# Rotary position step of a gated Mamba and MoE block: the halves of queries and keys change places by SBUF transfers instead of a TensorE product

## The chip, the cores and the metric

The kernel runs on one core of one Trainium2 chip. The metric is the time of one execution in microseconds (us), as the device measures it; the median of several runs is given. The engines of the core are TensorE (PE in the profile; PEld is its weight load), VectorE (DVE), ScalarE (ACT), GpSimd (POOL) and SyncE (SP), which here only issues DMA transfers (SPq). Each engine works through its own list of instructions in order, and waits on semaphores.

## The reference

Four sequences of 512 tokens with 512 channels go through two stages, each behind a tanh gate:

```
x = x + tanh(g_xattn) * mamba(ctx, z=layernorm(x))     # 16 states, 512 channels
x = x + tanh(g_ffn)   * block(layernorm(x))
block(x):
    h = rms(x) ;  q = h@wq + bq ;  k = h@wk + bk ;  v = h@wv + bv     # 16 heads of 32
    q, k = q*cos + rot(q)*sin, k*cos + rot(k)*sin     # rot(t) = concat(-t2, t1), halves of 16
    x = x + causal_attention(q, k, v) @ wo
    x = x + MoE(rms(x))        # 8 experts, top 2, and a shared expert
```

`rot` is the step that changes: within each head of 32 channels the first 16 and the last 16 change places, one of them with its sign turned.

## The kernel before

The program is written engine by engine: five functions, one for each engine, list its instructions, and counting semaphores join them. There is no scheduler; the order in the text is the order on each engine.

After `first_scan` (the Mamba scan of sequence 0) there are four rounds, `round_(b, s)` with b = 0 to 3 and s = b + 1. Round b does the attention of sequence b and, in rounds 0 to 2, the scan of sequence s beside it. Round 3 has no scan; it does the first pieces of the shared expert instead (`last_units`). Then the MoE stage follows.

Within a round there are three stretches: norms and transposes; then the **rotary stretch**, a loop over eight tiles m = 0 to 7 (four of queries, four of keys, each 128 channels by 512 tokens, so four heads in the partitions); then the 16 `units` of attention with the 64 scan blocks spread between them. The rotary stretch is where the change lies. For each tile m, in the kernel before:

- PE `product(b, m)`: 12 matmuls of line 631 into one of two PSUM banks;
- ACT `bias(b, m)`, line 1296: adds the bias and writes the tile into `QB[:, m % 2]`, one of two buffers (in `EX`), once tile m - 2 has been rotated;
- PE `rotate(b, m)`, line 749: a float32 product with the permutation `perm`, which puts channel d in the place of channel d xor 16, into PSUM bank `A[m % 2]`; the profile lists it as two matmuls;
- POOL `rope_cos(b, m)`, line 2313: `QB` times the cosine table into `RC` (in `PT`);
- DVE `rope_out(b, m)`: line 1816 multiplies the rotated tile by the sine table (whose first half carries the sign) into `RS`, line 1820 adds `RC` and writes `QK[:, m]`.

In rounds 0 to 2 pieces of the scan's preparation stand between them: PE `du_term`, `turn_c` and `delta` (line 689) after products 0 to 3; DVE `delta_relu` (line 1746) after `rope_out` 1 and 2, and `delta_sum` and `delta_u` (lines 1752 and 1758) after `rope_out` 4 and 5; ACT `delta_exp` after bias 4 and `delta_log` (line 1259) after bias 5; POOL `driven(s, 0)` (line 2281) between `rope_cos` 6 and 7. PE `delta(s, 3)`, which stands ahead of product 4, waits for the second `delta_relu`. In round 3 DVE has `low_gate_up` (line 2036) after `rope_out` 5.

The stretch ends where PE `scores(b, 0)` (line 762) may start, after `rope_out` 7 has written `RS`, and where DVE's first `scan` (line 1770) starts in rounds 0 to 2; that stands behind the last `rope_out` on DVE and needs POOL's `driven` too.

SP issues all ordinary transfers. In a round it stores the scan's B rows (line 504), loads two rows of them broadcast over the partitions (`load_b_row`, line 441) and then has nothing to do until the units. In round 3 it loads the shared expert's weights (lines 445 and 449) and the parts of sequence 0 kept in DRAM (line 522) ahead of the rotary stretch, and those of sequence 1 (line 525) after the eighth product.

## Time and profile before

| | us |
|---|---|
| median of three runs | 1789.75 |
| lowest and highest | 1787.08 and 1792.86 |
| the profiled execution | 1790.59 |
| its span in the trace | 1788.8 |

| stretch (from the span's start) | us |
|---|---|
| rotary stretch of rounds 0, 1, 2 (first product to first scan block) | 190.3 to 234.6, about 436 to 481.7, about 685 to 730.8 |
| rotary stretch of round 3 (first product to first scores) | 928.5 to 962.2 |

The profile gives each engine's busy time, and in rows of the form start, duration, engine, line, operation, tiles, what ran when. A bracket at a row's end gives how long the engine had been idle before it and what released it. For a matmul the end is modelled, so the distance between two starts is the better measure of what one costs. Rows of SPq are the issue of a transfer; the data come later, and the table of DMA issues has the time from issue to landing.

### The profile page before, as it was taken

The page shows a single profiled execution, that of the slowest core. Times are in us where ns is not written, and L with a number is a line of the kernel's source. Part 1 is how long each engine was busy: PE and PEld are TensorE (multiplying, and loading weights), DVE is VectorE, ACT ScalarE, POOL GpSimd, SP SyncE. Part 2 cuts the span into 40 slices and gives each one's busy share as a digit, 9 for nine tenths or more (in the row PEclk, how much of TensorE's full clock was granted, in tenths as well). Part 3 has the DMA queues.
Part 4 walks back from the last instruction along what each step waited for, and adds up shares of the span by engine and source line. Part 5 has one row for each costly group of instructions (what it writes and reads, how often), then busy time and mean ns, then how long its engine had stood idle before and what let it go on. Part 6 is the DMA issues. An engine that isn't in the chain of part 4 may idle for free.

```text
span 1788.8 us, 26797 instructions
## 1 busy us (share of the span) xinstructions
PE 1503.7 (84%) x9168; PEld 1150.6 (64%) x9168; DVE 1166.9 (65%) x1699; ACT 916.2 (51%) x2038; POOL 810.2 (45%) x807
## 2 busy tenths in 40 slices
PE   5677967788777789677878998799999999999994
PEld 2344645565445556455655666688787999999973
DVE  5987589996699985899945444432324666566545
ACT  5675457764467753567724663221213666666510
POOL 1992266542466532565413211243422555555444
PEclk8789968899878899788988999899999999999997
DMA  4460001111011111011132004721311877777464
GB/s 168 153 229 19 25 23 55 54 43 54 7 35 55 54 36 31 19 47 54 37 123 95 30 32 160 293 77 59 110 37 65 307 243 253 261 241 253 155 221 165
DMA packets 94664, 195.76 MB, mean 109 GB/s; under 512 B 8945, under 2 KB 25841, under 8 KB 91201
## 3 DMA queue, kind: packets, MB, share of 16 engines
q1 hardware_dynamic: 89408, 177.26, 29.1%
q0 software_dynamic: 5120, 16.78, 2.8%
q8 instruction: 75, 1.23, 0.3%
q14 instruction: 61, 0.49, 0.1%
HBM read 140.40 MB, written 53.61 MB: 108 GB/s over the span
## 4 chain that ended last, share of the span: by engine, by line
PE 55%; DVE 16%; issue 15%; POOL 7%; ACT 5%; DMA 1%; SPq 1%; DVEq 0%; ACTq 0%; POOLq 0%
PE scores L631 21%; PE bank L631 14%; DVE HS L1770 6%; DVE YA L1781 4%; PE bank L705 3%; PE bank L775 3%; POOL GB L2281 2%; PE bank L790 2%; ACT bank L1269 2%; PE bank L825 2%; PE scores L762 2%; POOL yab L2471 2%; PE scores L749 1%; PE bank L1092 1%; PE scores L765 1%
## 5 line engine op out<-in xcount | busy, mean ns | idle before, releaser
L2281 POOL TENSOR_TENSOR GB<-DU,BB 128x512 f32<-128x512 f32 x256 | 326.8, 1298 | 36.1 <-DVE DL L1752 21.2
L1770 DVE TENSOR_TENSOR_SCAN HS<-bank,GB 128x512 f32<-128x512 f32 x224 | 272.0, 1214 | 20.3 <-ACT bank L1269 17.6
L705 PE MATMUL bank<-ident,HS 128*128 128x128 f32 x860 | 165.8, 325 | 120.9 <-DVE YA L1781 104.9
L705 PEld LDWEIGHTS bank<-ident,HS 128*128 128x128 f32 x860 | 115.2, 165 | 166.3 <-DVE YA L1781 129.8
L1269 ACT ACTIVATE bank<-DL,aneg 128x512 f32<-128x512 f32 x224 | 154.7, 691 | 110.0 <-DVE HS L1770 108.2
L775 PE MATMUL bank<-ident,EX 128*128 128x128 f32 x640 | 131.5, 306 | 34.2 <-ACT PT L1314 20.9
L631 PE MATMUL scores<-xth,wgh 128*128 128x256 f32 x552 | 158.1, 286 | 2.2 <-DVE fa L2162 1.3
L1781 DVE SCALAR_TENSOR_TENSOR YA<-bank,Ct,YA 128x512 f32<-128x512 f32 x199 | 147.0, 738 | 14.2 <-PE bank L705 12.8
L631 PE MATMUL scores<-xth,wgl 128*128 128x256 f32 x552 | 156.1, 283 | 0.0
L631 PE MATMUL scores<-xtl,wgh 128*128 128x256 f32 x552 | 156.1, 283 | 0.0
L1314 ACT ACTIVATE PT<-bank 128x128 f32<-128x128 f32 (+3 forms) x256 | 110.3, 431 | 72.0 <-PE bank L775 64.9
L1306 ACT ACTIVATE EX<-scores,nm 128x128 f32<-128x128 f32 (+3 forms) x256 | 132.3, 521 | 22.4 <-DVE nm L1826 21.7
L775 PEld LDWEIGHTS bank<-ident,EX 128*128 128x128 f32 x640 | 79.8, 154 | 75.0 <-issue 47.0
L2426 POOL TENSOR_TENSOR wgl<-wgr,wgh 128x768 fp32r<-128x768 f32 x54 | 110.9, 2057 | 30.4 <-ACT wgh L1580 30.4
L2443 POOL TENSOR_TENSOR fal<-fa,fah 128x512 fp32r<-128x512 f32 x30 | 38.8, 1293 | 162.7 <-ACT fah L1609 162.5
L2324 POOL TENSOR_TENSOR ctl<-cn,cth 128x128 fp32r<-128x128 f32 x64 | 29.3, 458 | 180.7 <-ACT cth L1325 180.7
L631 PEld LDWEIGHTS scores<-xth,wgh 128*128 128x128 f32 x552 | 105.7, 191 | 3.6 <-DVE fa L2162 1.7
L631 PE MATMUL scores<-hah,wgh 128*128 128x512 f32 x272 | 106.7, 392 | 1.0 <-issue 1.0
L631 PE MATMUL scores<-hal,wgh 128*128 128x512 f32 x272 | 106.5, 391 | 0.0
L631 PE MATMUL scores<-hah,wgl 128*128 128x512 f32 x272 | 106.3, 391 | 0.0
L631 PEld LDWEIGHTS scores<-xtl,wgh 128*128 128x128 f32 x552 | 105.7, 192 | 0.9
L631 PEld LDWEIGHTS scores<-xth,wgl 128*128 128x128 f32 x552 | 105.7, 191 | 0.0
(294 smaller groups left out, 3798.6 us busy)
## 6 DMA issues: line engine op xcount, KB each, us to landing
wgr<-wffn_in SPq DMA_DIRECT2D x108, 384.0 KB, 6.5
wdr<-wffn_in SPq DMA_DIRECT2D x81, 256.0 KB, 3.1
BB<-b_scratch SPq DMA_DIRECT2D x64, 256.0 KB, 3.3
xr<-xg SPq DMA_DIRECT2D x23, 512.0 KB, 5.8
yg<-ysb SPq DMA_DIRECT2D x23, 512.0 KB, 6.5
xg<-V SPq DMA_DIRECT2D x11, 1024.0 KB, 5.8
hah<-hhd SPq DMA_DIRECT2D x5, 1024.0 KB, 14.1
hal<-hhd SPq DMA_DIRECT2D x5, 1024.0 KB, 16.1
```

The costliest lines, as they stand in the source:

```text
L631: mm = nc.tensor.matmul(out_, parts[a](k), rhs_parts[b](k), start=(k == 0 and j == 0), stop=(k == n - 1 and j == 2))
L705: mm = nc.tensor.transpose(state_bank(s, q)[:, et * P:(et + 1) * P], HS[:, n % 2, et, tt * P:(tt + 1) * P], ident[:])
L762: nc.tensor.matmul(SB[:, a, 0:W], QK[r:r + HD, m, i * P:(i + 1) * P], QK[r:r + HD, 4 + m, 0:W], start=True, stop=False)
L775: mm = nc.tensor.transpose(turned_bank(b, v)[:, kb * P:(kb + 1) * P], EX[:, a, kb * P:(kb + 1) * P], ident[:])
L1269: nc.scalar.activation(decay_bank(s, k), DL[:, et, :], ACT.Exp, scale=aneg[:, et, n:n + 1]).then_inc(dA_ready, 1)
L1306: nc.scalar.activation(EX[:, a, 0:W], SB[:, a, 0:W], ACT.Exp, bias=nm[:, a:a + 1], accum_out=rs[:, q % 2, a:a + 1]).then_inc(ex_done, 1)
L1314: nc.scalar.activation(PT[:, a, 0:W], turned_bank(b, v)[:, 0:W], ACT.Copy).then_inc(pt_done, 1)
L1770: nc.vector.tensor_tensor_scan(HS[:, n % 2, et, :], decay_bank(s, k), GB[:, k % 4, :], 0.0, ALU.mult, ALU.add).then_inc(scan_done, 1)
L1781: nc.vector.scalar_tensor_tensor(YA[:, tt, :], state_bank(s, q), Ct[:, tt, n:n + 1], YA[:, tt, :], ALU.mult, ALU.add).then_inc(y_acc, 1)
L2281: nc.gpsimd.tensor_tensor(GB[:, k % 4, :], DU[:, et, :], BB[:, n % 2, :], ALU.mult).then_inc(gb_ready, 1)
L2426: nc.gpsimd.tensor_tensor(wgl[raw][:, c, :], wgr[raw][:, c * 2 * EW:(c + 1) * 2 * EW], wgh[raw][:, c, :].bitcast(f32), ALU.subtract).then_ ...
L2443: nc.gpsimd.tensor_tensor(fal[:, b % 2, c, :], fa[:, s % 2, :], fah[:, b % 2, c, :].bitcast(f32), ALU.subtract).then_inc(f_al, 1)
```

## The change

`rotate` goes. In its place SP issues eight transfers for each tile, from SBUF to SBUF: each moves 16 partitions of `QB` (2 KB in each, 32 KB in all) to the neighbouring group of 16 partitions of a new buffer `QR`, which lies in the half of `PT` that this stretch leaves free. Line 1816 on DVE then reads `QR` in SBUF and no longer PSUM. Two semaphores (`rot_in`), one for each buffer, count the transfers; a tile is there when its semaphore has risen by 128. `bias` m + 2 waits for that where it waited for the rotation. Before each tile SP waits for the bias of the tile and for line 1816 of tile m - 2, which frees `QR`.

```
+        QR = PT[:, 2:4]
...
+            def swap_halves(b, m):
+
+                sp.wait_ge(qb_ready, 8 * b + m + 1)
+                at(sp, rope_s, 8 * b + m - 1)
+                for j in range(P // (HD // 2)):
+                    to, of = [slice(i * HD // 2, (i + 1) * HD // 2) for i in (j, j ^ 1)]
+                    sp.dma_start(QR[to, m % 2, :], QB[of, m % 2, :]).then_inc(rot_in[m % 2], 16)
...
                     for n in range(2):
                         load_b_row(s, n)
+                    if b >= 0:
+                        for m in range(8):
+                            swap_halves(b, m)
...
                     for j, part in enumerate((rows_hi[0], rows_lo[0])):
                         sp.dma_start(part.bitcast(f32), hhd[j, 0]).then_inc(hh_ld[0], 16)
+                    for m in range(8):
+                        swap_halves(b, m)
                     sp.wait_ge(qk_mm, 2 * T4 * B)
...
-            def rotate(b, m):
-                pe.wait_ge(qb_ready, 8 * b + m + 1)
-                if m < 2:
-                    pe.wait_ge(v_done, T4 * b + m + 1)
-                else:
-                    pe.wait_ge(rope_s, 8 * b + m - 1)
-                nc.tensor.matmul(A[m % 2][:], perm[:], QB[:, m % 2, :], start=True, stop=True).then_inc(rot_mm, 1)
...
                 for m in range(8):
                     if att:
                         product(b, m)
-                        if m:
-                            rotate(b, m - 1)
...
             def bias(b, m):
                 act.wait_ge(qk_mm, 8 * b + m + 1)
                 if m >= 2:
-                    act.wait_ge(rot_mm, 8 * b + m - 1)
+                    act.wait_ge(rot_in[m % 2], 128 * (4 * b + m // 2))
                     act.wait_ge(rope_c, 8 * b + m - 1)
...
                 f = SCALE if m < T4 else 1.0
-                dve.wait_ge(rot_mm, 8 * b + m + 1)
+                dve.wait_ge(rot_in[m % 2], 128 * (4 * b + m // 2 + 1))
...
-                nc.vector.scalar_tensor_tensor(RS[:, m % 2, :], A[m % 2][:], f, rope[:, 1, :],
+                nc.vector.scalar_tensor_tensor(RS[:, m % 2, :], QR[:, m % 2, :], f, rope[:, 1, :],
```

The semaphore `rt_split` is merged with `consts`, with the same waits under other counts. The load of `perm` stays.

On SP, the list of round 0 around its loads of B rows. The first fence is the kernel before, the second the changed one; `PT<-EX` are the transfers from `QB` to `QR`, eight for each of eight tiles.

```order
L504 DMA b_scratch<-xd 16x512
L433 DMA cT<-ctx_in 128x1024
L441 DMA BB<-b_scratch 128x512 x8
L487 DMA x2d<-xa 128x512
L441 DMA BB<-b_scratch 128x512
```

```order
L513 DMA b_scratch<-xd 16x512
L434 DMA cT<-ctx_in 128x1024
L442 DMA BB<-b_scratch 128x512 x2
L490 DMA PT<-EX 16x512 x64
L442 DMA BB<-b_scratch 128x512 x6
```

The 64 transfers stand between the second load of a B row and the third, which belongs to the units.

On SP in round 3, the weights (`wgr`, `wdr`) and the stored parts of sequences 0 and 1 (`hhd`), in the changed kernel:

```order
L534 DMA wah<-hhd 128x4x512
L534 DMA wal<-hhd 128x4x512
L490 DMA PT<-EX 16x512 x64
L539 DMA wal<-hhd 128x4x512 x2
L543 DMA xs_early<-x2d 128x2048 x2
```

The 64 stand behind two loads of 1 MB and ahead of four more.

On PE in round 0, after the last three matmuls of product 2. Before, tile 1 is rotated there; now `turn_c` follows at once.

```order
L631 MATMUL bank<-h1h,wah 128x512
L631 MATMUL bank<-h1l,wah 128x512
L631 MATMUL bank<-h1h,wal 128x512
L749 MATMUL scores<-EX,perm 128x512
L676 MATMUL bank<-ident,xd 128x48 x4
L689 MATMUL bank<-xd,dtproj 128x512 x2
```

```order
L645 MATMUL bank<-h1h,wah 128x512
L645 MATMUL bank<-h1l,wah 128x512
L645 MATMUL bank<-h1h,wal 128x512
L690 MATMUL bank<-ident,xd 128x48 x4
L703 MATMUL bank<-xd,dtproj 128x512 x2
```

The rotation's place is empty; nothing else on PE has moved.

## Rows read from the trace of the kernel before

**Rows 1.** The page, busy time by engine: share of the span, instructions.
```profile
PE 1503.7 (84%) x9168; PEld 1150.6 (64%) x9168; DVE 1166.9 (65%) x1699; ACT 916.2 (51%) x2038; POOL 810.2 (45%) x807
```

**Rows 2.** Timeline, PE, round 0: start, duration, engine, line, operation, tiles, count.
```profile
219.42 1.02 PE L749 MATMUL scores<-EX,perm 128*128 128x512 f32 x2
...
223.03 1.02 PE L749 MATMUL scores<-EX,perm 128*128 128x512 f32 x2
```

**Rows 3.** Timeline, PE, round 3: the first matmul of products 0 and 1.
```profile
928.50 0.39 PE L631 MATMUL bank<-h1h,wah 128*128 128x512 f32 x1
...
931.22 0.39 PE L631 MATMUL bank<-h1h,wah 128*128 128x512 f32 x1
```

**Rows 4.** Timeline, ACT, round 0: bias 0, bias 4, the four logarithms.
```profile
197.78 0.67 ACT L1296 ACTIVATE EX<-bank,bqk 128x512 f32<-128x512 f32 x1
...
216.01 0.69 ACT L1296 ACTIVATE EX<-bank,bqk 128x512 f32<-128x512 f32 x1 [2.26 <-PE bank L631]
...
221.62 2.19 ACT L1259 ACTIVATE GB<-GB 128x512 f32<-128x512 f32 x4
```

**Rows 5.** Timeline, DVE, round 0, tiles 1, 4 and 7 and what follows.
```profile
205.09 0.69 DVE L1816 SCALAR_TENSOR_TENSOR EX<-scores,rope 128x512 f32<-128x512 f32 x1 [3.18 <-PE scores L749]
...
207.24 1.61 DVE L1746 TENSOR_SCALAR DL<-bank,chan 128x512 f32<-128x512 f32 x2 [0.43 <-ACT GB L1250]
...
220.48 0.69 DVE L1816 SCALAR_TENSOR_TENSOR EX<-scores,rope 128x512 f32<-128x512 f32 x1 [1.86 <-PE scores L749]
...
231.71 0.68 DVE L1816 SCALAR_TENSOR_TENSOR EX<-scores,rope 128x512 f32<-128x512 f32 x1
233.02 1.67 DVE L1820 SCALAR_TENSOR_TENSOR QK<-PT,EX 128x512 f32<-128x512 f32 x1 [0.63 <-POOL PT L2313]
234.60 1.21 DVE L1770 TENSOR_TENSOR_SCAN HS<-bank,GB 128x512 f32<-128x512 f32 x1
```

**Rows 6.** Timeline, SP: issues in a row at the start, later, and by ones.
```profile
4.97 0.43 SPq L460 DMA_DIRECT2D dtproj<-dtproj_in  x1
5.44 1.85 SPq L437 DMA_DIRECT2D xa<-x_in  x4
...
33.33 2.21 SPq L437 DMA_DIRECT2D xa<-x_in  x4
...
1096.91 0.36 SPq L550 DMA_DIRECT2D hah<-hhd  x1
```

**Rows 7.** DMA issues: count, KB each, median us from issue to landing.
```profile
h2d<-hp SPq DMA_DIRECT2D x16, 256.0 KB, 2.0
...
b_scratch<-xd SPq DMA_DIRECT2D x4, 32.0 KB, 1.6
...
dtproj<-dtproj_in SPq DMA_DIRECT2D x1, 32.0 KB, 2.5
```

**Rows 8.** Stretches: length, PE, PEld, DVE, ACT, POOL busy, PEclk, DMA share, GB/s.
```profile
232.50:235.50 3.00, 1.34 (x12) 0.85 (x12) 2.48 (x2) 0.00 (x0) 3.00 (x3) 0.50 0.00 0
...
452.00:458.00 6.00, 6.00 (x16) 3.68 (x14) 1.77 (x3) 1.97 (x3) 0.00 (x0) 0.72 0.00 0
...
932.00:938.00 6.00, 6.00 (x26) 4.43 (x25) 1.71 (x2) 1.15 (x4) 2.59 (x2) 1.00 0.82 302
938.00:944.00 6.00, 6.00 (x25) 4.46 (x24) 3.43 (x4) 2.60 (x4) 2.59 (x2) 1.00 0.01 3
```

**Rows 9.** Timeline, ACT, round 3: bias 0.
```profile
931.42 0.69 ACT L1296 ACTIVATE EX<-bank,bqk 128x512 f32<-128x512 f32 x1 [11.33 <-PE bank L631]
```

**Rows 10.** Timeline, DVE, round 3: tiles 5, 6 and 7.
```profile
953.04 0.69 DVE L1816 SCALAR_TENSOR_TENSOR EX<-scores,rope 128x512 f32<-128x512 f32 x1 [1.85 <-PE scores L749]
...
954.72 1.80 DVE L2022 TENSOR_SCALAR sg<-gs,tgq 128x8 f32<-128x8 f32 x1
...
959.23 0.68 DVE L1816 SCALAR_TENSOR_TENSOR EX<-scores,rope 128x512 f32<-128x512 f32 x1
...
961.45 0.68 DVE L1816 SCALAR_TENSOR_TENSOR EX<-scores,rope 128x512 f32<-128x512 f32 x1
```

More of the change, by code:

```diff
@@ L277, in build @@
         wah_done, wal_done = sem("att_weights_hi"), sem("att_weights_lo")
-        rt_split = sem("router_split")
         a_bn, a_mv, a_norm, a_hp = [sem("att_" + n) for n in ("stats", "meanvar", "norm", "scaled")]
@@ L281, in build @@
         v_mm, v_done = sem("v_product"), sem("v_ready")
-        qk_mm, qb_ready, rot_mm, rope_c, rope_s, qk_done = [sem(n) for n in
-                                                            ("qk_product", "qk_biased", "qk_rotated", "rope_cos", "rope_sin", "qk_ready")]
+        qk_mm, qb_ready, rope_c, rope_s, qk_done = [sem(n) for n in
+                                                            ("qk_product", "qk_biased", "rope_cos", "rope_sin", "qk_ready")]
+        rot_in = [sem(f"qk_halves_swapped{h}") for h in range(2)]
         s_mm, mx_done, ex_done = sem("scores_ready"), sem("row_max"), sem("exp_ready")
@@ L1013, in round_ @@
                             delta(s, 2 * m - 3)
-                if att:
-                    rotate(b, 7)
                 if att and scn:
@@ L1028, in _ @@
             pe.wait_ge(attc_in, 80)
-            pe.wait_ge(rt_split, 2)
+            pe.wait_ge(consts, 7 + T4 + 2)
             pe.wait_ge(wal_done, KC)
@@ L1699, in _ @@
             act.wait_ge(attc_in, 80)
-            nc.scalar.activation(rth[:], rtw[:], ACT.Copy).then_inc(rt_split, 1)
+            nc.scalar.activation(rth[:], rtw[:], ACT.Copy).then_inc(consts, 1)
             for r in range(B):
@@ L2242, in _ @@
             dve.wait_ge(attc_in, 80)
-            dve.wait_ge(rt_split, 1)
-            nc.vector.tensor_tensor(rtl[:], rtw[:], rth[:].bitcast(f32), ALU.subtract).then_inc(rt_split, 1)
+            dve.wait_ge(consts, 7 + T4 + 1)
+            nc.vector.tensor_tensor(rtl[:], rtw[:], rth[:].bitcast(f32), ALU.subtract).then_inc(consts, 1)
             dve.wait_ge(zfill, 16 * 12)
```

## The prediction

> **What bounds the kernel now.** I read the page's first part for the load of each engine, then the timelines of the rotary stretch engine by engine, then the table of DMA issues, since the change trades a product for transfers. PE is the busiest engine, with 84% of the span [rows 1], so taking work from it looks like a gain. Whether it is one depends on what ends each rotary stretch. The reader should follow the chain from the last tile back.
>
> In round 0 the stretch ends with the first scan block at 234.60. It stands behind the last addition of tile 7 (233.02), that behind the sine product of tile 7 (231.71), and DVE has been at work with no idle time shown since then [rows 5]. PE had given tile 4 at about 220.4, and DVE takes 14.1 us from there (220.48 to 234.60) for four tiles and the scan's softplus terms between them. So in rounds 0 to 2, which are alike, DVE is late at the end and not PE. At the start of the units TensorE's granted clock is 0.50, its lower level of 1.2 GHz, after it had stood idle [rows 8]; the units begin slowly today already.
>
> In round 3 nothing of a scan is there. PE goes from one product to the next without a gap (6.00 us busy of 6.00, clock 1.00 [rows 8]) and sets the pace of the tiles up to number 5. DVE then sets the end: from the sine product of tile 5 (953.04) to that of tile 7 (961.45) are 8.4 us, with the low parts of the shared expert's weights in between [rows 10].
>
> **What is removed.** With a rotation, two starts of it on PE lie 223.03 - 219.42 = 3.61 us apart in the tail of the stretch [rows 2], where one product and one rotation make up the distance. A product without one is 931.22 - 928.50 = 2.72 us from its first matmul to the next product's [rows 3]. A rotation is then 0.89 us, and 32 of them are 28.5 us of PE's 1503.7 [rows 1]. Of that next to nothing is on the path in rounds 0 to 2, as DVE ends those. In round 3 it would be worth up to 7 us if the new way to turn a tile kept up with 2.72 us per tile. It doesn't, as follows.
>
> **What is added.** Eight issues per tile on SP, 256 in all. SP is otherwise idle there, and no other engine waits for anything queued behind them: the next B row belongs to the units, and in round 3 the loads for sequence 1 are used much later. What each issue costs when it follows another is in the trace: the 16-partition transfer `dtproj` took 0.43 us and the next began 0.47 after it; four loads took 1.85, or 0.46 each; in a crowded stretch four took 2.21, or 0.55 each; one that followed a single issue took 0.36 [rows 6]. I take 0.475 with the gap, by the row of the same 16-partition size, and keep 0.40 (0.36 and a gap of 0.04) and 0.60 (0.55 and a gap) as ends. A tile costs SP 8 x 0.475 = 3.80 us, and 0.06 for its waits: 3.86. This is more than a product and more than product and rotation together, so the new pacemaker of the tiles is SP.
>
> From issue to landing no SBUF-to-SBUF transfer is in the trace. The nearest are a 16-partition store of 32 KB from SBUF to DRAM at 1.6 us, a store of 256 KB at 2.0, and the 16-partition load of 32 KB at 2.5, with other loads ahead of it [rows 7]. I take 1.8, between the two stores, since a queue with a few small transfers in it is nearer to them, and keep 1.6 and 2.5. A tile is there 7 x 0.475 + 1.8 = 5.1 us after its first issue.
>
> The Trainium skill, "DMA: Bandwidth & Descriptors", section "Rules for kernel authors", says of many small transfers that they should be merged into one large one, as below 64 KB one pays mostly overhead. The rows agree in kind: eight times the bytes cost 0.4 us more. By the same page's fit (section "Anatomy of one DMA", given for transfers issued by GpSimd), a fixed 2.0 us and the bytes over 436 GB/s, 32 KB would take 2.1; with that landing the sum below would be about 3 us higher.
>
> **Round 0 step by step.** Bias 0 ends at 197.78 + 0.67 = 198.45 [rows 4]; ACT is late there for reasons the change leaves alone. With a pace of 3.86 the first issues of tiles 0 to 3 are at 198.5, 202.4, 206.2 and 210.1, and they land at 203.6, 207.5, 211.3 and 215.2. Tile 1's sine product was at 205.09 and is now at 207.5. Behind it on DVE stand the two `delta_relu`, which were at 207.24 [rows 5]; they end at about 210.9 now, after 0.69, about 1.0 for the addition, and 1.61. PE's fourth `delta` waits for them, so product 4 starts at about 211.9, ends at 214.6, and bias 4 starts at 214.7, where it was at 216.01 [rows 4]. That is all that PE's lighter work brings. Tile 4 is issued from 215.4 on and lands at 220.5 to 220.6; its sine product was at 220.48 [rows 5]. The logarithms ran at 221.62 and come earlier, as bias 5 does. From here DVE's own 14.1 us count as before. Tile 5 lands 3.86 later at 224.5 and tile 6 at 228.3, both ahead of their turn, and tile 7 at 232.1, where its turn would be 231.9. The last addition also waits for POOL, which runs 0.1 to 0.2 later. The first scan block moves from 234.60 to about 234.9: **+0.3 us**, and +1.0 for the three rounds. The ends: with issues at 0.40 and landing at 1.6 tile 4 is there about 1.7 us earlier, and each round gains 1.3. With a landing of 2.5 the delay counts twice (through `delta_relu` to bias 4, and again on tile 4), and tile 7 adds to it: +2.6. With 0.60 per issue a tile takes 4.86, tile 7 is there near 237, and a round loses 5.
>
> **Round 3.** Bias 0 ends at 931.42 + 0.69 = 932.1 [rows 9]. The queues are still full then (0.82 of their time, 302 GB/s) and empty after 938 [rows 8], so the first transfers land near 938, and their issues may cost 0.55 instead of 0.475 for these six us: eleven of them, 1.0 us in all. Bias 2 waits for tile 0 until 938, which does not yet hold up SP. Tile 5 lands at 932.1 + 5 x 3.86 + 5.1 + 1.0 = 957.5, where its sine product was at 953.04. Behind it on DVE come the weights' low parts, and the whole chain to tile 7 shifts with it: +4.4. Tile 7 itself lands at 932.1 + 27.0 + 5.1 + 1.0 = 965.2, before its new turn at 965.9. The scores shift by **+4.2**, with a little off, because POOL meets DVE less there. The ends are -0.5 (issues at 0.40) and +10 (0.60).
>
> **Sum.** +1.0 + 4.2 = +5.2 us on the profiled 1790.59, thus 1795.8; on the median of the three runs, which is 0.8 lower, 1795.0, or +0.29%. About 0.3% (5.4 us) is what a measurement of this kernel can tell from no change, and the forecast lies just below that edge. The lower end is 3 x -1.3 - 0.5 = -4.4, the upper one from the landing alone 3 x 2.6 + 5 = +13, from 0.60 per issue 3 x 5 + 10 = +25.
>
> **Rivals.** First, **the queue keeps up** (faster): SP issues 16-partition transfers as fast as 0.36 each [rows 6] and PE's lighter work shows. At 0.37 with its wait a tile takes SP 3.0 us, and round 3 turns into a gain too: three rounds of -1.7 and one of -1.2, so about -6, 1784. Against it: the 16-partition `dtproj` itself took 0.43. Second, **the queue is slower than its rows** (slower): transfers between two groups of partitions land later than stores, or issues in long runs cost 0.55 and more, as in the crowded row [rows 6]. From about 0.49 per issue, or 1.9 of landing, it decides for slower. In its middle, 0.55 with 2.0, rounds 0 to 2 lose 4 each and round 3 loses 8: +20, 1810. Third, **the clock**: between products PE now waits about 1.1 us per tile, where it was busy throughout. The trace shows that the clock can fall inside this very stretch (0.72 on average from 452 to 458, all of it busy [rows 8]). At the lower level a product takes twice 2.72, more than SP's 3.86, and PE is late. One such fall per round costs up to 2 us each time: +8 on top, 1803. That stretches of 1.1 us would be enough to drop it to 1.2 GHz for the whole stretch I hold unlikely; it would cost over 10 us a round. That the rotation does not leave TensorE, or comes back elsewhere, is excluded by the order of instructions: the product is gone and the 256 transfers are there.
>
> **Chances.** Queue as in its rows, the forecast: 0.60 (faster than -0.3% 0.02, within 0.38, slower 0.20, as the landing decides). Queue keeps up: 0.09, all faster. Queue slower: 0.21, all slower. Clock: 0.10, of which 0.02 within 0.3%. So faster 0.11, within 0.3% 0.40, slower 0.49; the likeliest case's own range is 1785 to 1803. The range of 1785 to 1811 leaves out the fast rival and the upper part of the slow one, near 0.2.
>
> **What would show it.** Right: 256 issues of SP on one line, 0.43 each and 0.475 apart in a run, about 1.8 us from issue to landing; bias m + 2 released by a DMA from tile 3 on; tile 7's sine product 0.3 to 0.7 later in rounds 0 to 2 and about 4.4 later in round 3; the units and the MoE stage of unchanged length. The forecast is wrong if issues lie 0.40 apart or less, if the landing is over 2.2, if the clock in the stretch is below 0.95 in rounds 0 and 3, or if the units change their length by more than 1 us.

## The result, and the profile after

The changed kernel takes 1820.38 us (median of 4 runs, 1819.43 to 1827.39), the kernel before 1788.9 (1787.08 to 1792.86): a ratio of 1.0183, with a 95% interval of 1.0160 to 1.0207. It is 31.5 us slower. The forecast was 1795.0, with a range from 1785 to 1811. Each experiment below has runs of the kernel before taken beside it (medians 1787.9 to 1788.9), and its ratio is against those. One run of the kernel before (3354.51 us) and one of the kernel with one transfer for each tile (2079.93 us) stand far above all others of the same kernel and are left out of the ratios.

The page of the changed kernel: span, busy time by engine, shares of the chain that ended last, and the new row of the DMA issues.

```profile
span 1818.7 us, 26923 instructions
...
PE 1475.8 (81%) x9104; PEld 1137.0 (63%) x9104; DVE 1158.0 (64%) x1699; ACT 914.9 (50%) x2038; POOL 809.3 (44%) x807
...
PE 50%; DVE 17%; issue 13%; SPq 7%; POOL 6%; ACT 5%; DMA 1%; DVEq 0%; ACTq 0%; POOLq 0%
...
PT<-EX SPq DMA_DIRECT2D x256, 32.0 KB, 2.0
```

Against [rows 1] PE has lost 1503.7 - 1475.8 = 27.9 us of work, as foreseen (28.5), and the kernel is longer all the same. SPq, the issuing of transfers by SP, has 7% of the span in the chain, where it had 1% before. What one issue takes is on the line that issues them (count; shortest, median and longest in ns; who waited for it, us and times; then issue to landing):

```profile
L490 SPq DMA_DIRECT2D PT<-EX x256: 507/589/1389, 199.2 to 990.1; - x128
...
  DVE EX L1818: 96.3, 29
  ACT EX L1298: 10.6, 3
...
DMA to landing us min/median/max: 1.9/2.0/5.5
```

and what a row of them takes is on SP's timeline of round 0 (start, duration, count at the end):

```profile
199.17 41.29 SPq L490 DMA_DIRECT2D PT<-EX  x64
242.65 0.33 SPq L442 DMA_DIRECT2D BB<-b_scratch  x1
```

SP is at it for 41.29 us of a stretch of 45.3. The median issue lasts 0.589 us and the next one starts 0.632 after it, where [rows 6] have 0.43 and 0.47. A tile is 8 x 0.632 = 5.06 us, not 3.86. Round 3, where no scan is mixed in, shows it as a drum beat. These are the starts of the sine products on DVE, with the idle time ahead of each and what ended it:

```profile
966.59 0.69 DVE L1818 SCALAR_TENSOR_TENSOR EX<-PT,rope 128x512 f32<-128x512 f32 x1 [3.64 <-DMA PT<-EX]
...
971.65 0.69 DVE L1818 SCALAR_TENSOR_TENSOR EX<-PT,rope 128x512 f32<-128x512 f32 x1 [3.63 <-DMA PT<-EX]
...
976.70 0.69 DVE L1818 SCALAR_TENSOR_TENSOR EX<-PT,rope 128x512 f32<-128x512 f32 x1 [3.63 <-DMA PT<-EX]
...
992.08 0.69 DVE L1818 SCALAR_TENSOR_TENSOR EX<-PT,rope 128x512 f32<-128x512 f32 x1 [3.04 <-DMA PT<-EX]
```

They are 5.05 us apart and each was released by a transfer. Before, they were released by PE until tile 5, and the last one stood at 961.45 [rows 10], 30.03 after bias 0; now it is 992.08 - 949.36 = 42.72 after it. PE waits for the chain at the end (timelines of ACT and PE, round 3, the first bias and the first scores):

```profile
949.36 0.69 ACT L1298 ACTIVATE EX<-bank,bqk 128x512 f32<-128x512 f32 x1 [11.31 <-PE bank L645]
...
992.88 0.81 PE L768 MATMUL scores<-QK 32*128 32x128 f32 x8 [15.83 <-DVE EX L1818]
```

The time by stretches, in us, worked out from such starts (bias 0 of a round to its first scan block, in round 3 to the first scores; then from there to bias 0 of the next round, in round 3 to the last copy of a transposed tile):

| | round 0 | round 1 | round 2 | round 3 |
|---|---|---|---|---|
| rotary stretch before | 36.8 | 38.4 | 38.4 | 30.8 |
| rotary stretch after | 45.3 | 45.0 | 45.2 | 43.5 |
| units and next preparation before | 208.7 | 210.7 | 200.6 | 124.9 |
| units and next preparation after | 207.3 | 207.7 | 200.4 | 123.8 |

The four rotary stretches are 34.6 us longer; 5.7 us come back between them. The whole loss is in the stretches that the change touches, and SP accounts for it. In round 0, from bias 0 (198.48): 0.69 until its first issue, 40.7 to its last, 1.97 until that one lands, and 1.94 of DVE's work (from 241.87) to the first scan block, 45.3 together.

In rounds 0 and 1 the chain of waits does not run along SP alone, though. This is the one of round 0 from the landing of tile 1 to bias 4 (start, duration, what):

```profile
209.02 1.97 DMA PT<-EX
212.35 0.76 DVE DL L1748
213.14 2.01 PE bank L703 x4
215.16 4.48 PE bank L645 x12
219.66 0.70 ACT EX L1298
```

This is the path that the prediction walked: tile 1 lands, DVE does its sine product (211.01) and `delta_relu`, PE its last `delta` and product 4, ACT bias 4. Product 4 takes 4.48 us here; 2.72 is the distance of such a product in [rows 3]. The stretches of 7 us around it (columns as in [rows 8]) show the clock:

```profile
199.00:206.00 7.00, 6.24 (x34) 4.58 (x34) 0.66 (x2) 3.21 (x7) 2.55 (x2) 1.00 0.19 42
206.00:213.00 7.00, 5.66 (x14) 3.61 (x14) 2.97 (x5) 2.44 (x5) 1.27 (x2) 0.76 0.23 52
```

TensorE's granted clock was 1.00 and then 0.76 on average, which is 2.4 GHz for a part and 1.2 GHz for the rest, and it is 0.76 again from 213 to 220. The first half of product 4 ran at the lower level. The chain of round 1 has 4.55 us for the same twelve matmuls. So product 4 became 1.7 us longer, but the stretch did not, because SP was not yet free. These are its issues of tiles 3 and 4:

```profile
214.76 5.43 SPq L490 DMA_DIRECT2D PT<-EX  x8
220.38 4.93 SPq L490 DMA_DIRECT2D PT<-EX  x8
```

Tile 3 was issued until 220.19, bias 4 ended at 220.35 and tile 4 began at 220.38. The chain names whatever came last, and not by how much: here it was by 0.16 us, in round 1 SP stood idle for 0.43 us, and in round 2, where product 4 ran at full speed, not at all. The fall of the clock cost some 0.5 us in the four rounds together.

Nor is it shown that the waiting for SP brought the fall. Before, product 3 of rounds 1 and 2 took 4.2 us from its first matmul to its last, in round 1 at a mean clock of 0.72 and with PE busy throughout [rows 8], while that of round 0 took 2.6. This is why round 0 was 36.8 us long before and rounds 1 and 2 38.4; with transfers in round 3 alone, round 0 has such a fall too, and is 38.5 us long.

The new form has one more cost. The sine product on DVE reads `QR` in SBUF now. Before, reading PSUM, none of the 32 took more than 0.70 us, though 28 began while POOL was working. Now 8 of 32 take 0.94 to 1.78 us. Each of them began while POOL was working, and lasted as long as POOL's instruction had left and 0.55 us more. Two rows of round 0, tiles 6 and 7:

```profile
236.82 1.78 DVE L1818 SCALAR_TENSOR_TENSOR EX<-PT,rope 128x512 f32<-128x512 f32 x1 [1.10 <-DMA PT<-EX]
241.87 1.30 DVE L1818 SCALAR_TENSOR_TENSOR EX<-PT,rope 128x512 f32<-128x512 f32 x1 [1.59 <-DMA PT<-EX]
```

Only the last tile's is on the path here, with 0.6 us. It counts for more where SP is quick, as an experiment below shows.

### The profile page after: what moved, and what is told of

Its sections match the earlier page's. It is cut to its first block, busy times and chain, and to the rows that moved or that the text cites. A ratio compares the mean times of both kernels' runs of the same rounds, so it can differ in the third digit from the quotient of the medians.

```text
span 1818.7 us, 26923 instructions
## 1 busy us (share of the span) xinstructions
PE 1475.8 (81%) x9104; PEld 1137.0 (63%) x9104; DVE 1158.0 (64%) x1699; ACT 914.9 (50%) x2038; POOL 809.3 (44%) x807
## 4 chain that ended last, share of the span: by engine, by line
PE 50%; DVE 17%; issue 13%; SPq 7%; POOL 6%; ACT 5%; DMA 1%; DVEq 0%; ACTq 0%; POOLq 0%
PE scores L645 21%; PE bank L645 12%; SPq L490 7%; DVE HS L1772 6%; DVE YA L1783 4%; PE bank L719 3%; PE bank L781 3%; PE bank L831 2%; PE scores L768 2%; PE bank L796 2%; POOL GB L2283 2%; ACT bank L1271 2%; POOL yab L2473 2%; PE bank L1094 1%; DVE nm L1828 1%
## 5 line engine op out<-in xcount | busy, mean ns | idle before, releaser
L781 PE MATMUL bank<-ident,EX 128*128 128x128 f32 x640 | 129.1, 302 | 30.0 <-ACT PT L1316 22.7
L768 PE MATMUL scores<-QK 32*128 32x256 f32 (+3 forms) x512 | 65.2, 588 | 65.9 <-DVE EX L1818 63.2
```

Source lines behind the costliest of these rows:

```text
L768: nc.tensor.matmul(SB[:, a, 0:W], QK[r:r + HD, m, i * P:(i + 1) * P], QK[r:r + HD, 4 + m, 0:W], start=True, stop=False)
L781: mm = nc.tensor.transpose(turned_bank(b, v)[:, kb * P:(kb + 1) * P], EX[:, a, kb * P:(kb + 1) * P], ident[:])
```

## Experiments

### What an issue costs, measured by itself

The kernel before, with nine series of transfers behind its last store, on SP, each series waited for before the next. One of them:

```
for j in range(8):
    go(dst[16*j:16*j+16, :], src[16*(j^1):16*(j^1)+16, :])   # within SBUF, 32 KB each
landed()
```

> The kernel before, and behind its last store nine series of transfers with nothing else running, each series waited for: eight of 16 partitions x 512 from SBUF to SBUF (groups changed, then 64 columns only), eight of 16 partitions SBUF to DRAM, eight DRAM to SBUF, four of 32 partitions SBUF to SBUF, four of 128 partitions x 128, three single ones of 128 x 512, four of 128 x 128 to DRAM and from DRAM. The profiled execution will be some 60 us longer; only the issue durations and landings are read. Theory 1 (the issue of a transfer whose both ends lie in SBUF is dear by its form): about 0.59 us for every SBUF-to-SBUF issue, whatever its partitions and bytes, and 0.43 or less for those with an end in DRAM. Theory 2 (16 partitions are dear): 0.59 for all four series of 16 partitions, 0.43 for 32 and 128. Theory 3 (the issue waits for data of the transfers ahead, so it is a matter of load in the kernel): 0.43 or less for all here, and less for 64 columns than for 512.

The time by itself says nothing (1831.25 us, with 42 us of series). SP's timeline of six of the series, in this order: within SBUF eight of 32 KB and eight of 4 KB; eight to DRAM; eight from DRAM; within SBUF four of 64 KB and four of 128 partitions by 128 columns:

```profile
1785.77 5.04 SPq L630 DMA_DIRECT2D xs_early<-xs_early  x8
...
1792.20 4.93 SPq L630 DMA_DIRECT2D xs_early<-xs_early  x8
...
1798.29 3.58 SPq L630 DMA_DIRECT2D yg<-xs_early  x8
1803.13 3.54 SPq L630 DMA_DIRECT2D xs_early<-yg  x8
...
1808.10 2.42 SPq L630 DMA_DIRECT2D xs_early<-xs_early  x4
...
1811.94 2.46 SPq L630 DMA_DIRECT2D xs_early<-xs_early  x4
```

Eight within SBUF take 5.04 us, eight with one end in DRAM 3.58 or 3.54. In a row these are 0.632 and 0.463 from start to start. The bytes hardly matter: 4 KB each, 4.93; 64 KB each, four in 2.42. The landings of the same series:

```profile
xs_early<-xs_early SPq DMA_DIRECT2D x8, 32.0 KB, 2.0
yg<-xs_early SPq DMA_DIRECT2D x8, 32.0 KB, 1.7
...
xs_early<-xs_early SPq DMA_DIRECT2D x8, 4.0 KB, 1.7
```

So the 0.43 of [rows 6] was right for what it showed, a load from DRAM. The form within SBUF, which no row of before had, costs 0.17 us more for each issue, and is neither a matter of a crowded queue nor of this kernel's waits.

An issue of more than 0.6 us did stand in the trace of before, with another form. These are the stores of transposed blocks, 128 partitions by four pieces of 128 columns, from SBUF to DRAM:

```profile
1084.15 0.52 SPq L494 DMA_DIRECT2D hhd<-h2h  x1
1084.72 0.64 SPq L494 DMA_DIRECT2D hhd<-h2l  x1
```

So the kind of ends is not all that sets the price. That rows of the same trace ran to 0.64 was reason enough for an upper end above 0.60.

### Fewer issues for the same bytes

Four transfers of 32 partitions in place of eight of 16, and one of 128, with the halves left where they are, so the change of places is left out of both:

```
-for j in range(P // (HD // 2)):
-    to, of = [slice(i * HD // 2, (i + 1) * HD // 2) for i in (j, j ^ 1)]
-    sp.dma_start(QR[to, m % 2, :], QB[of, m % 2, :])...
+for j in range(P // HD):
+    rows = slice(j * HD, (j + 1) * HD)
+    sp.dma_start(QR[rows, m % 2, :], QB[rows, m % 2, :])...
```

> The changed kernel with four transfers of 32 partitions for each tile instead of eight of 16; they leave out the change of places (each group goes to its own place), all waits and bytes are as in the changed kernel. Theory 1 (eight issues one after another on SP, 0.632 us apart, set the pace of the tiles): a tile costs SP 4 x 0.632 = 2.6 us, less than PE's product, so the stretch falls back to the other engines: rounds 0 to 2 about 2 us shorter than before each, round 3 about 2.5 shorter, 1780 in all, 40 below the changed kernel. Rival (the round trip of a transfer, 2.0 us to landing and its waits, is what costs): the same number of round trips remains, so still 1805 to 1818.

Measured 1789.58 us (1788.25 to 1791.56), ratio 1.0002 (0.9993 to 1.0012). Halving the issues gives back the whole loss of 31 us, with the same bytes and the same PE work. What it doesn't give is the gain of 8; the next kernel shows why.

> The changed kernel with one transfer of 128 partitions for each tile, again without the change of places. Theory 1: a tile costs SP 0.65 us; every round's stretch is bound by PE's products, ACT and DVE: 3 us shorter than before in rounds 0 to 2 and 5 in round 3, 1774 to 1780. It is also the upper bound for what taking the rotation from PE can bring. Rival (round trip): 1800 or more. A second rival (VectorE reading the turned tile from SBUF is slowed by GpSimd): rounds 0 to 2 no shorter than before.

Measured 1786.01 us (median of 10 runs), ratio 0.9985 (0.9975 to 0.9995). This is what taking the rotations from PE brought by this route at its quickest: 2.7 us and not 14. Rounds 1 and 2 got 2.4 shorter (36.0), round 0 0.7 longer, and round 3 only 1.8 shorter. In round 3 the first tile was issued at 930.05 and its sine product began at 937.3, behind the loads of the shared expert's weights and of the stored parts of sequence 0. The others then follow 2.3 us apart, faster than any before.

Where the rest of the 14 went, DVE's timeline of round 1 shows, with the sine products of tiles 4, 6 and 7 and the first scan block:

```profile
463.56 0.69 DVE L1816 SCALAR_TENSOR_TENSOR EX<-PT,rope 128x512 f32<-128x512 f32 x1 [3.14 <-DMA PT<-EX]
...
473.67 1.75 DVE L1816 SCALAR_TENSOR_TENSOR EX<-PT,rope 128x512 f32<-128x512 f32 x1
...
477.01 1.75 DVE L1816 SCALAR_TENSOR_TENSOR EX<-PT,rope 128x512 f32<-128x512 f32 x1
...
480.38 1.21 DVE L1770 TENSOR_TENSOR_SCAN HS<-bank,GB 128x512 f32<-128x512 f32 x1
```

From tile 4 to the scan DVE needs 480.38 - 463.56 = 16.8 us, in each of rounds 0 to 2, where it needed 14.1 before [rows 5] for the same instructions. Two of the four sine products take 1.75 in place of 0.68, and each of the 10 of 32 that are longer than 0.8 us in this kernel again lasted as long as POOL's instruction had left, and some 0.55 us. Tile 4 came earlier (19.2 us after bias 0 in place of 24.3 in round 1), and 2.7 of that went to DVE. The expectation had this as its second rival, VectorE slowed by GpSimd, and the traces bear it out in kind: with its operand in SBUF and no longer in PSUM, the product waits for POOL, on the engine that ends the stretch. No run tested this by itself. Round 0, 0.7 longer, has a fall of the clock in product 3 on top (4.2 us from first matmul to last).

DVE sets the end of the stretch in all four rounds, and that the prediction had read rightly from before.

### Transfers without anyone waiting

The kernel before with its rotations on PE, and the same 256 transfers on SP beside them (the same row counts, 128 columns each), which nobody in the stretch waits for; only ScalarE's third copy of the units does:

```
+for m in range(8):
+    for j in range(8):
+        sp.dma_start(QR[rows, m % 2, cols], V[rows, 2 + m % 2, cols]).then_inc(zfill, 16)
```

> The kernel before, with its rotation on PE, and beside it 64 transfers per round from SBUF to SBUF (16 partitions, 128 columns) which SP issues in the rotary stretch into the buffer that the changed kernel uses; only ScalarE's third copy of turned probabilities waits for them, which stood 6 us behind the end of the stretch. Theory 1 (the cost is in the wait for the issues, not in their presence): 1789 to 1796, the little that the last of them reach past the stretch. Rival (256 transfers slow the engines by contention for SBUF or the queues): 1805 to 1820.

Measured 1791.43 us (1788.22 to 1793.45), ratio 1.0012 (1.0001 to 1.0022). That is 2.7 us, by the interval 0.2 to 3.9, and a wait has its part in it. The rotary stretches are no longer than before (36.8, 36.9, 38.5 and 30.8 us). In round 3 SP was at its 64 issues until 968.40, and ScalarE's copy waited for the last of them; the units there took 3.9 us more:

```profile
927.38 41.02 SPq L492 DMA_DIRECT2D PT<-V  x64
969.67 0.28 ACT L1330 ACTIVATE PT<-bank 128x128 f32<-128x128 f32 x1 [3.81 <-issue]
```

So the mere presence of the 256 transfers, with a quarter of the bytes, costs nothing that this run shows. The 31 us are waiting.

### Which rounds pay

Transfers in round 3 only, and in rounds 0 to 2 only; the other rounds rotate on PE as before:

```
+D = b in (3,)            # or (0, 1, 2)
 dve.wait_ge(rot_in[...]) if D, else dve.wait_ge(rows_made, ...)
 scalar_tensor_tensor(RS[:, m % 2, :], QR[:, m % 2, :] if D else A[m % 2][:], ...)
```

> The halves change places by transfers in the last attention round only; in rounds 0 to 2 TensorE turns them, as before. If the whole loss is SP's issue pace (eight issues 0.632 us apart are 5.06 us for each tile, where a tile of products leaves TensorE every 2.72 us in this round), the round grows from 30.8 to 43.5 us as it did with transfers in all rounds, rounds 0 to 2 stay at 36.8, 38.4 and 38.4 us, and about 1 us comes back after it: 1801 us (1799 to 1803). If the loss of round 3 came from what earlier rounds left behind (SP late, the queue filled), it is smaller here: below 1796 us.

Measured 1801.33 us (1798.02 to 1805.19), ratio 1.0066 (1.0044 to 1.0087): +12.9, as expected. Its round 3 is 43.9 us long, the other three 38.5.

> The halves change places by transfers in rounds 0 to 2 only; in the last round TensorE turns them. By the same theory the three rounds grow by 8.5, 6.6 and 6.8 us, the units and the preparation after them give 4 to 5 us back at a higher granted clock, and round 3 stays at 30.8 us: 1806 us (1804 to 1810). This and the run with transfers in round 3 alone then add up to the whole loss of 31.6 us. If the rounds only delay work that has slack, it is under 1800 us.

Measured 1818.33 us (1816.33 to 1821.08), ratio 1.0165 (1.0133 to 1.0197): +29.9 where 17 were expected. The rotary stretches did what they should: 46.1, 45.0 and 45.6 us, 23.0 longer together, and 30.8 in round 3. The two rotary sums, 23.0 and 13.1, add up to 36.1 against 34.6 in the changed kernel. The medians don't: 12.9 + 29.9 = 42.8 against 31.5. The difference lies in stretches that no edit touches. One is the third of units and preparation, in the changed kernel and in this one:

```profile
749.00:949.00 200.00, 147.66 (x1144) 106.58 (x1141) 166.50 (x218) 122.70 (x315) 99.65 (x117) 0.82 0.16 52
...
752.00:955.00 203.00, 153.68 (x1144) 111.96 (x1142) 167.04 (x217) 123.35 (x316) 99.78 (x117) 0.79 0.16 51
```

The same 1140 matmuls are busy for 6 us more at a clock of 0.79 against 0.82. Over the profiled kernels of this study the units of round 1 took between 206.8 and 210.9 us with equal instructions in them, and all that follows the attention 700.9 to 705.4 (the kernel with the series left out). What decides when the clock falls in a stretch that isn't changed stays open, and with it whether the 3 to 6 us that the units "gave back" in the changed kernel belong to the change. The kernel with the series at its end, whose instructions up to there are those of before, also had 206.8 in round 1 where before had 210.7, so at least that part does not.

### The prediction with its own pace

Eight transfers for each tile at the same places with the same waits, but to DRAM, where an issue starts 0.463 us after the one before. The sine product reads what the tile holds, so the change of places is left out:

```
-sp.dma_start(QR[to, m % 2, :], QB[of, m % 2, :]).then_inc(rot_in[m % 2], 16)
+sp.dma_start(swp[m % 2, to, :], QB[of, m % 2, :]).then_inc(rot_in[m % 2], 16)
```

> Eight transfers of 16 partitions for each tile as in the changed kernel, at the same places with the same waits, but they go to a buffer in DRAM; the sine product reads whatever the tile of turned halves holds, so the change of places is left out. Eight such issues stood 0.463 us apart where they were measured alone, against 0.632 within SBUF: 3.70 us for each tile, which is the pace that the prediction took. If its sum was right but for the pace, rounds 0 to 2 grow by 0 to 3 us each and round 3 by 3 to 5 us, some of it comes back, and the time is 1796 us (1792 to 1801). If the loss lies in what the transfers do to others or in the longer row of waits, and not in the pace, it stays above 1810 us.

Measured 1794.64 us (1789.55 to 1799.54), ratio 1.0027 (1.0012 to 1.0042). The rounds grew by 1.1, -0.8, 0.2 and 3.2 us; the prediction had 0.3 for each of the first three and 4.2 for the last. Its round 3 beats as the sum assumed:

```profile
948.00 0.69 DVE L1818 SCALAR_TENSOR_TENSOR EX<-PT,rope 128x512 f32<-128x512 f32 x1 [2.29 <-DMA swp<-EX]
...
951.70 0.69 DVE L1818 SCALAR_TENSOR_TENSOR EX<-PT,rope 128x512 f32<-128x512 f32 x1 [2.28 <-DMA swp<-EX]
```

3.70 us from tile to tile. With the pace that was assumed, the predicted time comes out; with 0.17 us more for each of the 64 issues that stand in a row in each round, and 0.3 more for each landing, another 26 are lost. The next run keeps the dear issues with the short landing, and so tells the two apart.

That every round agrees within 1.1 us is luck in part. Bias 0 to tile 4's sine product took 22.1 and 21.8 us in rounds 0 and 1, where before it took 22.7 and 24.3 (a fall of the clock in round 1), and from there DVE took 15.8 where the sum had 14.1. The one makes up for the other.

### Eight small transfers

As the changed kernel, each transfer with 64 of its 512 columns, so most of the change of places is left out:

```
-sp.dma_start(QR[to, m % 2, :], QB[of, m % 2, :])
+sp.dma_start(QR[to, m % 2, 0:64], QB[of, m % 2, 0:64])
```

> Eight transfers within SBUF for each tile, at the places and with the waits of the changed kernel, but each moves 64 columns of its 16 rows (4 KB) in place of 512 (32 KB), so most of the change of places is left out. If SP's pace alone costs, 0.632 us from issue to issue whatever an issue moves, the time is that of the changed kernel less a few tenths of a microsecond for each landing (1.7 against 2.0 us where both were measured alone): 1819 us (1816 to 1822), and round 3 takes 43 us or a little more. If the bytes or the load on the 16 DMA engines had a part in it, it falls by 3 us or more below 1820.

Measured 1823.78 us (1819.13 to 1824.39), ratio 1.0188 (1.0171 to 1.0205). An eighth of the bytes and a landing of 1.7 in place of 2.0 bring nothing back (round 3: 43.2 us); the time is 1.8 us above what was expected. The bytes are free here and the 0.3 us of landing are too; the issues are not.

### Two engines share the issues

The whole computation; SP issues four of a tile's eight, ScalarE the other four behind its bias add:

```
+act.wait_ge(qb_ready, 8 * b + m + 1)
+for j in range(P // HD, 2 * P // HD):
+    nc.scalar.dma_start(QR[to, m % 2, :], QB[of, m % 2, :]).then_inc(rot_in[m % 2], 16)
```

> The whole computation with all eight transfers, four issued by SP and four by ScalarE behind its bias add. If the pace is the issuing engine's own, a tile's eight issues take 4 x 0.632 = 2.53 us on each of the two; ScalarE, busy 17.8 of 38.5 us in rounds 0 to 2 and 10.1 of 30.8 in round 3, takes 20 us of issues more in each round: nearly full in rounds 0 to 2, where its later bias adds and gates come up to 2.5 us late. Most of the 31 us comes back: 1795 us (1788 to 1803). If the issues of both engines pass one place that takes 0.632 us for each, the pace of a tile stays 5.06 us and the time is 1818 us or more.

Measured 1834.79 us (1832.03 to 1838.26), ratio 1.0253 (1.0236 to 1.0270), 40 us above the first theory. By its number alone it falls under the second (1818 or more), but the trace shows something else. ScalarE's timeline at the start of round 0:

```profile
199.83 0.67 ACT L1298 ACTIVATE EX<-bank,bqk 128x512 f32<-128x512 f32 x1
200.53 2.52 ACTq L1304 DMA_DIRECT2D PT<-EX  x4
203.15 1.09 ACT L1226 ACTIVATE YA<-bank 128x512 f32<-128x512 f32 x2 [2.65 <-issue]
204.12 0.69 ACT L1298 ACTIVATE EX<-bank,bqk 128x512 f32<-128x512 f32 x1
204.84 2.70 ACTq L1304 DMA_DIRECT2D PT<-EX  x4
207.65 1.08 ACT L1226 ACTIVATE YA<-bank 128x512 f32<-128x512 f32 x2 [2.83 <-PE bank L683]
```

Four issues of ScalarE take 2.5 to 2.7 us (median of one 0.612) while SP issues its own four at the same time, at its usual 0.589 each: the pace belongs to the issuing engine, and two engines issue twice as much. Round 3 gains by it (37.3 us against 43.5), so "one place that all issues pass" falls. But in rounds 0 to 2 each stretch became 51 us long. Bias 1 came 1.5 us after bias 0 and now comes 4.3 after it, `YA` (which PE waits for at L683) comes 2.7 later, and so at each tile, for these stand behind ScalarE's own issues. The expectation had added up ScalarE's load (38 of 38.5 us) and had not asked who waits for it.

### By way of DRAM

The whole computation, three issues for each tile: the tile stored twice, 32 rows apart in blocks of 64, and one load that begins 16 rows into each block.

```
+for k in range(2):
+    to = AP(swp, 32*k*512, [[64*512, 4], [512, 32], [1, 512]])
+    sp.dma_start(to, QB[:, m % 2, :]).then_inc(zfill, 16)
+sp.wait_ge(zfill, 192 + 32 * (8 * b + m + 1))
+sp.dma_start(QR[:, m % 2, :], AP(swp, 16*512, [[64*512, 4], [512, 32], [1, 512]]))
```

> The whole computation: each tile is stored twice to DRAM (two issues) with its halves placed so that one load brings it back turned, three issues for each tile in place of eight. Issue pace theory: SP is busy with a tile for two stores (0.93 us), the landing of the stores (about 1.7 us) and one load (0.43 us), 3.1 us in all, which is less than the 3.80 us that TensorE leaves between tiles in rounds 0 to 2 and a little more than 2.72 us in round 3; a product waits about 5 us from its bias to the landed load instead of about 7: 1793 us (1788 to 1798), so most of the loss is gone though the bytes are three times as many. If bytes moved or the length of the chain from bias to landing are what costs, it is 1805 us or more.

Measured 2027.56 us, ratio 1.1327 (1.1294 to 1.1360), far above the 1793 of the pace theory. The rival ("the length of the chain from bias to landing", 1805 or more) has the right sign, for a reason that it did not name. SP's timeline in round 0, and a stretch of 2 us within it (DMA share and GB/s at the end):

```profile
200.28 1.26 SPq L491 DMA_DIRECT2D swp<-EX  x2
209.05 0.55 SPq L494 DMA_DIRECT2D PT<-swp  x1
...
220.41 0.54 SPq L494 DMA_DIRECT2D PT<-swp  x1
...
205.00:207.00 2.00, 2.00 (x9) 0.78 (x7) 0.00 (x0) 0.00 (x0) 0.00 (x0) 1.00 0.26 102
```

The issues are cheap, but the stores take about 8 us to land, since a share of 0.26 is 4 of 16 DMA engines. A tile takes 11 us. The Trainium skill, "DMA: Bandwidth & Descriptors", section "Why a DMA increments its semaphore by 16 and not by 1", says that a transfer is split over k engines, the largest k up to 16 that divides the size of the slowest dimension in both its patterns. The slowest dimension in DRAM has the size 4 here, and in SBUF 128, and the trace agrees (0.26 x 16 = 4.2). As a test, the same way with one store and one load of the plain tile, 128 rows on both sides, which leaves the change of places out:

> As the way through DRAM before, but each tile is stored once as it stands, in one pattern of 128 partitions, and loaded back in one such pattern, so the change of places is left out and the buffer in DRAM is written once. The two stores of that other kernel, whose pattern in DRAM was 4 blocks of 32 rows, were carried by about 4 of the 16 DMA engines (share 0.26) and took 8 us. If that pattern was the cause of its 2027 us, here the share is that of all engines for a moment, store and load land in about 2.3 us each, a tile's way is 0.5 + 2.3 + 0.5 + 2.3 = 5.6 us with SP held 3.3 us, and the time is 1791 us (1786 to 1798). If it was the way through DRAM as such (the load that waits for a landed store), the time is above 1850 us.

Measured 1797.69 us (1794.24 to 1802.22), ratio 1.0039 (1.0019 to 1.0058), as expected (1786 to 1798) and 230 us less than the other. The way through DRAM as such is not what cost; the pattern was. The landings:

```profile
swp<-EX SPq DMA_DIRECT2D x32, 256.0 KB, 2.5
...
PT<-swp SPq DMA_DIRECT2D x32, 256.0 KB, 2.7
```

Round 3 is 7 us longer than before here (37.8), as a tile's way is 0.5 + 2.5 + 2.7 us and more. Even with the halves turned for nothing this would not beat the kernel before. Of the kernels that do the whole computation, none that was run beats it.

## Why the prediction was wrong

**What bounds the kernel** was read rightly. DVE ends the rotary stretches of before, and the kernel with one transfer for each tile shows it: even with rotations gone from PE and hardly an issue on SP, 2.7 us are to be had. Two details were not: the row of the last addition shows DVE waiting 0.63 for POOL [rows 5], so it was not busy all the way, and rounds 0 to 2 were not alike, as rounds 1 and 2 had a fall of the clock that made them 1.6 longer.

**What is removed**: 28.5 us of PE's work predicted, 27.9 in the trace, next to nothing of it on the path. Right.

**The issue** is the term that failed. It decided the result. The mechanism was right: SP became the pacemaker of the tiles. The size was taken from `dtproj`, a load of the same 16 partitions, at 0.475 with its gap [rows 6]; it is 0.632. The range ended at 0.60, so the pace was outside even that. The row was chosen for its number of partitions, which has next to no influence (16, 32 or 128 partitions within SBUF: 0.63 to 0.65 apart), and differed in what has, the kind of both ends. The prediction said that no transfer between two places in SBUF was in the trace, bounded its landing for that reason, and did not do the same for its issue.

**The landing**: 1.8 assumed, 2.0 found (1.9 to 5.5, the longest in round 3 behind the loads, as foreseen), within the bounds.

**DVE's 14.1 us** "count as before" in the sum, and line 1816 kept its 0.69. No row showed that instruction with both operands in SBUF. With them there, DVE needs 15.8 us (to DRAM, eight issues) or 16.8 (one transfer) for the same work. In the changed kernel little of it shows, as DVE waits for SP most of the time: 0.6 us at the last tile.

**The sum from there** has the right form: SP's pace, the landing, then DVE. With its pace made true, by transfers to DRAM, the measured time was 1794.6 where 1795.0 was forecast, in part by luck, as said there. Its upper end was added up wrongly. At 0.60 for each issue, tile 7 is not "there near 237" in round 0 but at 198.5 + 7 x 4.86 + 7 x 0.60 + 1.8 = 238.5, so that a round loses nearly 7 and not 5, and the end is some 31 above and not 25. The end for a landing of 2.5 is 1.8 for a round by the same steps, and not 2.6. At the measured pace the steps give 198.5 + 7 x 5.06 + 7 x 0.632 + 1.8 = 240.1 for tile 7, 8.4 after its place before; round 0 lost 8.5. For round 3 they give 12.3 without the crowded queue, and it lost 12.7. This is the rival "the queue is slower than its rows" in full, whose middle was put at 0.55 and 1810, and whose chance was 0.21. The stated range stopped at 1811, below even the sum's own end for 0.60.

**The clock** was a rival of its own, "one such fall per round costs up to 2 us each time", at 0.10. The falls came, with product 4 at 4.48 and 4.55 us in rounds 0 and 1. The cost hardly did, 0.5 us in all: the rival weighed a slow product against SP's 3.86, and SP took 5.06. In round 3 the means were 0.73, 0.78 and 0.50 in the stretches of 6 us from 970 on, and it cost nothing, as a product at 1.2 GHz, with 0.43 us from matmul to matmul, takes about as long as SP's tile. At a pace of 3.70, with transfers to DRAM, product 4 of round 0 took 2.97 us.

**Rounds 1 and 2** lost 6.6 and 6.8 us where round 0 lost 8.5, since before they were longer by their fall of the clock, and after all three have the length that SP gives them, 45.

**The units** were to keep their length within 1 us. They came out 1.4 and 3.0 shorter in rounds 0 and 1, within what the same instructions do from one of these kernels to another.

## What to carry to other kernels

Where a change adds many small transfers, price the issue first: count the issues that stand in a row, and take their pace from a row with the same kinds of ends, or measure eight of them at the end of a kernel, which takes one run. When one term is "no such row in the trace", each thing it does (issue, landing, share of the engines) is unknown, not only the one that comes to mind; the same goes for an operand that moves from one memory to another. A chain of waits names who came last, not by how much: look how long the other one was still busy before a cost is put down to it. And before work is taken from the busiest engine, ask which engine ends the stretch: a gain of 2.7 us for the quickest form, measured first, would have ended this idea at once.

## What the runs showed of the hardware

- An issue by SP of a transfer within SBUF takes 0.589 us and 0.632 to the next; with one end in DRAM 0.420 and 0.463, in either direction. Partitions (16, 32 or 128) and bytes (4 to 64 KB) change it by about 0.01 us in these series. A store to DRAM in blocks of 128 columns took 0.64 all the same. The first after a wait is shorter in all series but the very first: 0.51 within SBUF, 0.30 to 0.34 with an end in DRAM; a whole tile within SBUF, issued alone, takes 0.46.
- VectorE's product of two tiles took 0.69 us with one of them in PSUM, beside POOL or not, and up to 2.28 with both in SBUF when it began while POOL was working: what POOL's instruction had left, and 0.55.
- ScalarE and SP issue at the same time at the same pace each (0.612 and 0.589 median).
- A transfer whose pattern in DRAM has 4 as its slowest dimension is carried by about 4 of the 16 DMA engines: 102 GB/s, 8 us for two stores of 256 KB, where a plain store of one lands in 2.5.
- With the same instructions in them, the units of round 1 took 206.8 to 210.9 us in the profiled kernels, at mean granted clocks of 0.86 to 0.82.
